# Four stacked attention and state-space layers on one core: every softmax hands on its eight heads in two halves of four

## The reference

```python
# layer 0: 16 heads of width 16, ONE key/value head, +-64 window, then a gate
p0 = softmax(where(window, (x Wq + bq)(ctx Wk + bk)^T / 4, -1e9)); a = (p0 v) Wo + bo
g = silu([a, x] Wg + bg); out = a*g + x*(1-g); x = rms(out)*rms_w; x = x - mean over tokens
# layer 1: three neighbouring context rows per token, squared-relu weights
w = relu(q . k_near)**2; x = x + (w / sum(w) . v_near) Wo^T
# layer 2: self-attention "sa", then cross-attention "ca": 16 heads of width 64, relative bias
x = softmax((q k^T + rel_bias) / 8) v Wo + bo + x          # k, v from x, then from ctx
# layer 3: a Mamba-2 block "m", then cross-attention "c3" of 8 heads of width 32
x = x + u @ out_proj ; x = x + softmax(q k^T / sqrt(32)) v Wo
```

## Time and profile before

| | |
|---|---|
| median of 3 runs | 1317.44 us (1317.29 to 1321.61) |
| the profiled execution: its time, its span | 1322.45 us, 1320.3 us |
| PE busy | 1254.7 us, 95% |
| PE weight loads | 1014.6 us, 77% |
| DVE busy | 866.9 us, 66% |
| ACT busy | 780.9 us, 59% |
| POOL busy | 320.5 us, 24% |
| mean granted TensorE clock | 0.982 |
| length of one pass of the loop, by the start of line 595 | 74.03 us |

### The profile page before, as it was taken

One profiled execution on the slowest core, in us unless ns is written; L12 is line 12 of the kernel. 1 busy time (PEld: TensorE's weight loads), 2 busy tenths in 40 slices (PEclk: granted clock), 3 DMA queues, 4 the chain that ended last, 5 costly groups with the idle time before them and its releaser, 6 DMA issues.

```text
span 1320.3 us, 28500 instructions
## 1 busy us (share of the span) xinstructions
PE 1254.7 (95%) x9842; PEld 1014.6 (77%) x9842; DVE 866.9 (66%) x3381; ACT 780.9 (59%) x2658; POOL 320.5 (24%) x750
## 2 busy tenths in 40 slices
PE   5787999999999999999999999999999999999877
PEld 3465778878878778878878788878878788877665
DVE  3645657767676767767676767767676767664533
ACT  3152746676585656676575656676575756655431
POOL 2104022231414122231414122231414131221220
PEclk8998999999999999999999999999999999999998
DMA  7810100101010100101010100101010100000000
GB/s 257 311 41 4 42 5 9 45 0 48 4 48 4 40 12 8 44 0 48 4 48 4 40 12 8 44 0 48 4 48 4 40 12 8 33 1 9 5 4 5
DMA packets 28592, 44.45 MB, mean 34 GB/s; under 512 B 4710, under 2 KB 20614, under 8 KB 28044
## 3 DMA queue, kind: packets, MB, share of 16 engines
q1 hardware_dynamic: 26252, 31.41, 7.2%
q0 software_dynamic: 2304, 12.58, 2.7%
HBM read 37.64 MB, written 6.34 MB: 33 GB/s over the span
## 4 chain that ended last, share of the span: by engine, by line
PE 89%; DVE 4%; ACT 3%; issue 1%; POOL 1%; DMA 1%; SPq 0%; DVEq 0%; POOLq 0%; another core or an unknown queue 0%
PE psum L501 57%; PE psum L495 11%; PE psum L661 5%; PE psum L680 5%; PE psum L550 3%; PE psum L713 2%; PE psum L570 1%; PE psum L760 1%; PE psum L726 1%; ACT sa_p L820 1%; PE psum L595 1%; ACT A L820 1%; PE psum L773 1%; PE psum L798 1%; DMA A<-in_rel 0%
## 5 line engine op out<-in xcount | busy, mean ns | idle before, releaser
L820 ACT ACTIVATE A<-A,small_ 128x128 f32<-128x128 f32 x384 | 148.4, 397 | 21.1 <-DVE small_ L1030 21.1
L812 ACT ACTIVATE A<-psum 128x1024 f32<-128x1024 f32 (+1 forms) x96 | 67.2, 699 | 100.6 <-PE psum L495 93.2
L1314 POOL TENSOR_SCALAR small_<-small_ 128x1 f32<-128x1 f32 x96 | 18.6, 193 | 436.6 <-DVE small_ L1044 327.3
L1030 DVE CUSTOM_DVE_ANT_0 A<-psum,cst 128x128 f32<-128x128 f32 x256 | 56.6, 286 | 90.1 <-PE psum L550 90.1
L495 PE MATMUL psum<-cst,A 128*128 128x128 f32 x608 | 93.3, 279 | 9.5 <-DVE A L1095 2.7
L820 ACT ACTIVATE sa_p<-sa_p,small_ 128x128 f32<-128x128 f32 x256 | 98.8, 393 | 3.1 <-DVE small_ L1030 3.1
L820 ACT ACTIVATE ca_p<-ca_p,small_ 128x128 f32<-128x128 f32 x256 | 98.7, 389 | 1.8 <-DVE small_ L1030 1.7
L1197 DVE SCALAR_TENSOR_TENSOR A<-psum,half_cw,A 128x127 f32<-128x127 f32 (+2 forms) x288 | 75.2, 340 | 32.8 <-ACT A L924 32.8
L1418 POOL TENSOR_TENSOR small_<-small_,neg_half 128x1 f32<-128x1 f32 x16 | 9.0, 565 | 326.1 <-DVE small_ L1228 326.1
L495 PEld LDWEIGHTS psum<-cst,A 128*128 128x128 f32 x608 | 68.5, 142 | 25.6 <-issue 4.4
L501 PEld LDWEIGHTS psum<-A,Wmi 128*128 128x128 f32 x640 | 74.1, 192 | 11.4 <-issue 11.3
(11 more groups left out here) (218 smaller groups left out, 3199.6 us busy)
## 6 DMA issues: line engine op xcount, KB each, us to landing
inT<-in_tokT SPq DMA_DIRECT2D x16, 256.0 KB
kv_rows<-A SPq DMA_DIRECT2D x16, 256.0 KB
ctx_in<-in_ctx SPq DMA_DIRECT2D x16, 128.0 KB, 2.0
A<-bias_rows SPq DMA_DIRECT2D x1, 2048.0 KB, 9.8
Wsakv<-in_wsa_kv SPq DMA_DIRECT2D x1, 2048.0 KB, 11.8
Wcakv<-in_wca_kv SPq DMA_DIRECT2D x1, 2048.0 KB, 11.8
ctx_end<-in_tokT SPq DMA_DIRECT2D x16, 128.0 KB
out<-x_out SPq DMA_DIRECT2D x16, 128.0 KB, 1.7
```

Of the source, the lines that this page charges most:

```text
L812: return act.activation(out, in_, ACT.Copy)
L820: ins = act.activation(p[:, h * T:(h + 1) * T], p[:, h * T:(h + 1) * T], ACT.Exp, scale=-1.0, bias=sm(part, "nm", w * HU + h, w * HU + h + 1),
L1030: ins = dve.tensor_tensor_reduce(p[:, at], scores[:, at], extra(h), 1.0, TOP, ALU.add, ALU.min, sm(PART[L], "nm", w * HU + h, w * HU + h + 1))
L1314: then(pool.tensor_scalar(t, src, scale, eps, ALU.mult, ALU.add))
```

## The change

Steps 3 to 6 above are done by four heads. ACT raises `exp` after the fourth and after the eighth head. DVE waits for the first half's `exp`, takes four reciprocals, multiplies 512 columns and raises `probs`, and then does the same for the second half. PE waits for each half's `probs`, transposes four heads and raises `PT`; ACT waits for each half's `PT` and copies 512 columns. `PTsb` is still raised once, after the second copy. `ORDER` and `SPARE` are as before.

```diff
-            def need_lows(t, L, w, half):
-                eng.wait_ge(sem[f"{L}_lows"], t.value(2, half + 1) if L == "c3" else t.value(4, 2 * w + half + 1))
+            def need_half(t, L, step, w, half):
+                eng.wait_ge(sem[f"{L}_{step}"], t.value(2, half + 1) if L == "c3" else t.value(4, 2 * w + half + 1))
...
+            def turn_halves(t, L, w, X, src):                       # PE
+                for half in range(2):
+                    need_half(t, L, "probs", w, half)
+                    at = slice(half * BANK, (half + 1) * BANK)
+                    turn(X[:, at], src[:, at], HU // 2).then_inc(sem[f"{L}_PT"], 1)
...
-                    need_unit(t, "l0_probs", w)
-                    turn(P_1, probs0[w], HU).then_inc(sem["l0_PT"], 1)
+                    turn_halves(t, "l0", w, P_1, probs0[w])
...
-                        need_unit(t, f"{L}_probs", w)
                         if w == 1:
                             need_unit(t, f"{L}_PTsb", 0)
-                        turn(X, (PA2, PB2)[w][L], HU).then_inc(sem[f"{L}_PT"], 1)
+                        turn_halves(t, L, w, X, (PA2, PB2)[w][L])
...
-                need(t, "c3_probs")
-                turn(P_4, probs3, HU).then_inc(sem["c3_PT"], 1)
+                turn_halves(t, "c3", 0, P_4, probs3)
...
                                          accum_out=sm(part, "sm", w * HU + h, w * HU + h + 1))      # ACT, softmax
-                ins.then_inc(sem[f"{L}_exp"], 1)
+                    if h % (HU // 2) == HU // 2 - 1:
+                        ins.then_inc(sem[f"{L}_exp"], 1)
+
+            def turned(t, L, w, to, X):                             # ACT
+                for half in range(2):
+                    need_half(t, L, "PT", w, half)
+                    at = slice(half * BANK, (half + 1) * BANK)
+                    ins = copy(to[:, at], X[:, at])
+                ins.then_inc(sem[f"{L}_PTsb"], 1)
...
-                rc, total = (sm(PART[L], name, w * HU, (w + 1) * HU) for name in ("rc", "sm"))      # DVE, softmax_norm
-                need_unit(t, f"{L}_exp", w)
-                then(dve.reciprocal(rc, total))
-                dve.tensor_tensor(heads(p), heads(p), each(rc, T), ALU.mult).then_inc(sem[f"{L}_probs"], 1)
+                for half in range(2):
+                    at = w * HU + half * HU // 2
+                    rc, total = (sm(PART[L], name, at, at + HU // 2) for name in ("rc", "sm"))
+                    need_half(t, L, "exp", w, half)
+                    then(dve.reciprocal(rc, total))
+                    here = heads(p[:, half * BANK:(half + 1) * BANK], HU // 2)
+                    dve.tensor_tensor(here, here, each(rc, T), ALU.mult).then_inc(sem[f"{L}_probs"], 1)
```

More of the change, by code:

```diff
@@ L386, in need_unit @@
                 eng.wait_ge(sem[name], t.n if name[:2] == "c3" else t.unit[w])
-            def need_lows(t, L, w, half):
-                eng.wait_ge(sem[f"{L}_lows"], t.value(2, half + 1) if L == "c3" else t.value(4, 2 * w + half + 1))
-            return need, free, need_unit, need_lows
+            def need_half(t, L, step, w, half):
+                eng.wait_ge(sem[f"{L}_{step}"], t.value(2, half + 1) if L == "c3" else t.value(4, 2 * w + half + 1))
+            return need, free, need_unit, need_half
         block = stack.enter_context(nc.Block())
@@ L489, in _ @@
             pe.sem_inc(sem["c3_kv"], 1)
-            need, free, need_unit, need_lows = need_by(pe)
+            need, free, need_unit, need_half = need_by(pe)
             def turn(out, src, n):
@@ L546, in run @@
                     else:
-                        need_lows(t, "l0", 0, 1)
+                        need_half(t, "l0", "lows", 0, 1)
                     for r in range(2):
@@ L556, in run @@
                     if w == 0:
-                        need_lows(t, "l0", 1, 1)
+                        need_half(t, "l0", "lows", 1, 1)
                     else:
                         need_unit(t, "l0_osb", 0)
-                    need_unit(t, "l0_probs", w)
-                    turn(P_1, probs0[w], HU).then_inc(sem["l0_PT"], 1)
+                    turn_halves(t, "l0", w, P_1, probs0[w])
                 return run
@@ L654, in run @@
                         if w == 1:
-                            need_lows(t, L, 0, 1)
+                            need_half(t, L, "lows", 0, 1)
                         else:
@@ L808, in _ @@
             act.wait_ge(sem["prep_done"], 2)
-            need, free, need_unit, need_lows = need_by(act)
+            need, free, need_unit, need_half = need_by(act)
             def copy(out, in_):
@@ L818, in softmax @@
                     if h % (HU // 2) == 0:
-                        need_lows(t, L, w, h // (HU // 2))
+                        need_half(t, L, "lows", w, h // (HU // 2))
                     ins = act.activation(p[:, h * T:(h + 1) * T], p[:, h * T:(h + 1) * T], ACT.Exp, scale=-1.0,
@@ L834, in run @@
                 def run(t):
-                    need_unit(t, "l0_PT", w)
-                    copy(PT0, P_1).then_inc(sem["l0_PTsb"], 1)
+                    turned(t, "l0", w, PT0, P_1)
                 return run
@@ L891, in moved, with moved_PT @@
                     return run
-                def turned(w):
+                def moved_PT(w):
                     def run(t):
-                        need_unit(t, f"{L}_PT", w)
-                        copy((Q2, K2)[w][L][:], X).then_inc(sem[f"{L}_PTsb"], 1)
+                        turned(t, L, w, (Q2, K2)[w][L], X)
                     return run
@@ L902, in layer2 @@
                         **{f"{L}_s{w}": [lambda t, w=w: softmax(t, L, w, (PA2, PB2)[w][L])] for w in range(2)},
-                        **{f"{L}_p{w}": [turned(w)] for w in range(2)}, f"{L}_m": [moved(PA2, f"{L}_oT", f"{L}_oT_sb")]}
+                        **{f"{L}_p{w}": [moved_PT(w)] for w in range(2)}, f"{L}_m": [moved(PA2, f"{L}_oT", f"{L}_oT_sb")]}
             def m_squares(t):
@@ L944, in turned3 @@
             def turned3(t):
-                need(t, "c3_PT")
-                copy(PT3, P_4).then_inc(sem["c3_PTsb"], 1)
+                turned(t, "c3", 0, PT3, P_4)
             def mixed3(t):
@@ L966, in _ @@
             steps = [0]
-            need, free, need_unit, need_lows = need_by(dve)
+            need, free, need_unit, need_half = need_by(dve)
             def step(ins):
@@ L1286, in _ @@
             steps = [0]
-            need_names, free, need_unit, need_lows = need_by(pool)
+            need_names, free, need_unit, need_half = need_by(pool)
             def restart():
```

## The result

The changed kernel takes **1321.36 us** (median of 20 runs, 1319.09 to 1328.26), the kernel before 1318.40 us (20 runs, 1316.29 to 1322.21): a ratio of 1.0028, 95% interval 1.0017 to 1.0038. It is 0.28% slower; 1317.7 was forecast, and the range, up to 1321.8, holds the value near its upper end. The profiled execution of the changed kernel took 1320.13 us (span 1318.3).

What follows compares the result with a forecast made beforehand. PE was taken to bound the loop, with shorter hand-overs helping only outside it. From the 1317.44 us median, edges -2.0 and loop +2.3 gave +0.3, so 1317.7 us, range 1312.8 to 1321.8.

Steps and rivals of the forecast that it cites:

- edge gain: Outside the loop: hand-overs in filling, the next phase, draining and closing sum to -2.0 us (bounds -3.1 to -0.7).
- loop loss: In the loop, PE starts `mix` of the second `sa` softmax 0.18 us later, 13 times: +2.3 us (bounds 0 to 4.7).
- rival E: Clock, at either end: moved gaps add or take one half-clock stretch, some 2 us either way, 1315.7 or 1319.7; chance 0.08.
- clock stretch less: Low end of the range: edges at -3.1 and one half-clock stretch fewer, giving 1312.8 us.
- margin: Loop, `sa_k` copy's end to PE's `mix` weight load: 0.22 us, of which 0.17 to 0.18 can absorb delay.
- The lower price for the added DVE work: DVE's halved normalising by the Trainium skill's fixed cost: two times 0.06 = 0.12 us added, not 0.29.
- filling and the next phase: Two hand-overs: `sa` in filling -0.45 us, the `sa_q` copy in the next phase -0.35 us.
- draining's normalising: Draining, at 1242.09: DVE is behind, so the halved normalising delays the path of `m` by +0.29 us.
- The opening: Two copies could gain 0.84 us before `kv_rows` is stored, but the gather's landing was taken as fixed: 0.
- Rival D: Loop, `sa` and `c3` corner: DVE, ACT, PE path bounds the pass, 0.54 us lost a pass, 1322.5 us; chance 0.10.
- B: The loop's margin holds, added delay below 0.17 us, pass stays 74.03: 1315.4 us; chance 0.26.
- C: The loop gains too, up to 0.95 us a pass: 1303.1 us, chance 0.04; small form 1311.5 to 1314, chance 0.08.

Runs made afterwards that it cites:

- e7: The changed kernel with 27 more spare matmuls in PE's idle gaps of the run-out (end of last phase, draining, closing): 1318.08 us, ratio to before 0.9996.
- e16: The kernel before with spare matmuls fitted to PE's idle gaps outside the loop: 1310.02 us, ratio to before 0.9930.
- e17: The changed kernel with the same fitted spare matmuls as e16: 1308.65 us, ratio to before 0.9922.
- e1: The kernel before, unchanged, run and profiled again: 1317.13 us, ratio to before 0.9984.
- e13: The changed kernel, unchanged, run and profiled again: 1322.89 us, ratio to before 1.0023.
- e2: Halves only for the exponentials' signal, reciprocals and normalising; PE's transposes and ACT's copy whole as in the kernel before: 1327.66 us, ratio 1.0043.
- e9: Halves only in the loop and the phase on either side of it, whole hand-overs at both ends: 1319.89 us, ratio to before 1.0010.
- e18: Halves everywhere but the loop, with fitted spare matmuls as in e16 and more in opening and filling: 1306.23 us, ratio to before 0.9901.

## Why the prediction was wrong

- **The forecast was +0.3 us, the change measured +3.0.** "Within 0.5%" held. That the sign came out as forecast is luck: +0.3 was the sum of an edge gain that came and a loop loss four times too large, and with the loop's true 0.65 it would have been -1.35.
- **The step that failed is the sum of the forecast, which has no term for the clock.** It stood apart as rival E, ±2 us with a chance of 0.08 and no direction. In its place the runs show a mean clock of 0.984 for 0.989, an estimated 12 us more at 1.2 GHz, and a cost of 2.96 + 1.35 = 4.3 us, which more than outweighs all the hand-overs. The cause is tested on both kernels: with spares in the run-out (e7) the changed kernel loses its 3 us of lag, and with the clock held (e16, e17) it is the faster one.
- **Rival E's price doesn't follow from its own figures.** Eight groups of eight transposes held back would be 8 x (1.95 - 1.09) = 6.9 us, not 2, and would have reached past the range; the low end's "clock stretch less" is a third figure, 1.5.
- **The base was wrong in the same way.** I compared with a profiled execution 5.0 us above the median and carried only a difference over. The clock row (0.94 in the run-out) was read as a property of the kernel. Over half of all executions of before (74 of 137) run at 0.990 or more. The base itself, 1317.44 of three runs, was 1.0 us under the median of twenty.
- **The loop: mechanism right, size off.** 0.05 a pass, not 0.18. DVE's added 0.26 reached ACT's exponentials as 0.17, since the lows had been started 0.42 after line 1103 before and start 0.33 after it now; the halved copy cost 0.05, not 0.07. The `sa_k` copy thus ends 0.22 later by its neighbours; less the 0.17 of margin that leaves 0.05. The lower price for the added DVE work that the prediction set beside its own, 0.12, was too low.
- **The edges: right.** Between e16 and e17 filling and the next phase gave 0.82 for 0.80, draining's normalising cost 0.17 for 0.29, its `c3` hand-over gave 0.70 for 0.52 and the closing one 1.03 for 0.95 (1.13 in the profiles of the two kernels). The whole is 1.8 in these traces and 1.4 in the times, where 2.0 - 0.65 = 1.35 follow from the terms.
- **The opening: not contradicted, hardly tested.** The gather began at 40.41 for 40.61, but the profiles of the same kernels differ by more than that: 39.73 in e1, 40.14 in e13. The store of `kv_rows` stood at 33.39 in the changed kernel's first profile and at 35.21 in e13, at 34.95 and 33.93 in the two of before, so its 1.6 us can't be put down to the change.
- **Rival D** had the place (the `sa` and `c3` corner) but not the wait: with halves on DVE alone PE waits on the product ahead of its second transposes, 0.25 us a pass (e2). The halves of PE remove it.
- **Rivals B and C:** no hand-over in the loop gained; B's 74.03 and C's under 73.8 were not seen, though at 0.05 a pass the loop came nearer to B than to the forecast.

Left open: why the change lowers the mean clock at all, why a given idle pattern falls in one execution and not in another (e9's run-out at 0.90, nearly all of it before's code), and which phase's halves lower it most. The single parts' intervals overlap.

## What to carry to other kernels

Before you price a hand-over in a stretch where the matmul engine isn't full, look at the granted clock of several executions, not of one profile, and at where in the program it falls; here the clock outweighed all seven softmaxes' hand-overs, and filling idle gaps with spare matmuls of the right length brought 0.7% to 1%, seven times what the change was worth. Where a halved producer met a whole consumer (e2), the producer's extra cost arrived in full: halve both or neither. Count a filler instruction by its time in the trace before placing it, and put it only where a gap stands in the same phase.

## What the runs showed of the hardware

- Idle gaps of PE of at most 1.8 us each, 2.4 us in sum, stood ahead of a fall to 1.2 GHz near 1243 us; the same sum in another split had none behind it in e1, and the run-out's clock differed between executions (0.95 and 0.97 before, 0.93 changed, 0.90 in e9).
- The time of the kernel before follows the mean clock of its execution by about 0.8 us for each 0.001 (137 executions, 1315.6 to 1324.8 us), but a stretch at 1.2 GHz in the first 20 us, where PE waited anyway, cost nothing that can be seen (e1). At a constant 1.000 five executions of e18 agree within 0.42 us.
- Halving a normalising of 1024 columns on DVE costs 0.26 us in the queue (1.63 for 1.37), halving its copy on ACT 0.05 us (1.05 for 1.00).
